# Conv pre-activation kernel (Hartley modes, then Sobel): edge sums one operation per chunk, half the pad cleared in pieces, one first-axis product moved

## The reference, cut to what matters

```python
# layer 0
x_ht = dht_2d(gn(x))                          # 128 x 128 Hartley transform, normalised per plane
out_modes = compl_mul2d(x_ht[:, :, :20, :20], weights1)   # sum over the input channels
x = x + idht_2d(zero_padded(out_modes))
# layer 1
g = gn(x)
gx, gy = depthwise_sobel(g)                   # 3 x 3, zero padding
x = x + sqrt(gx * gx + gy * gy + 1e-8)
```

## Time and profile before

| what | us |
|---|---|
| median of 3 executions | 2263.78 (2262.36 to 2263.88) |
| the profiled execution, its own time | 2263.11 |
| its span, first to last instruction | 2261.3 |
| PE busy | 2147.4 (95%) |
| ACT busy | 1960.1 (87%) |
| DVE busy | 1799.2 (80%) |
| POOL busy | 1631.3 (72%) |
| mean granted TensorE clock | 0.977 of full speed |

### The profile page before, as it was taken

How to read it: one execution, slowest core, us unless ns; L and a number is a source line. 1 busy time by engine, 2 the same in 40 slices (tenths; PEclk the granted TensorE clock), 3 DMA queues, 4 the chain that set the end, 5 groups by cost and what they waited for, 6 DMA issues and landing times.

```text
span 2261.3 us, 54772 instructions
## 1 busy us (share of the span) xinstructions
PE 2147.4 (95%) x20404; PEld 1564.9 (69%) x20404; DVE 1799.2 (80%) x2702; ACT 1960.1 (87%) x3688; POOL 1631.3 (72%) x931
## 2 busy tenths in 40 slices
PE   5999999999992789999999999999999999999998
PEld 4888888888882656666666666666666666666665
DVE  4888888888887558877877877877887887887777
ACT  5988889888884369899899899899899989989998
POOL 4777777677667257777777777777777777777776
PEclk9999999999996779999999999999999999999999
DMA  7777777777774216666566666666666666656664
GB/s 214 216 204 211 205 207 207 206 207 208 201 188 84 75 57 189 176 196 193 176 195 188 181 192 187 186 182 192 186 186 187 191 182 193 193 176 190 199 190 137
DMA packets 808226, 414.62 MB, mean 183 GB/s; under 512 B 20784, under 2 KB 807216, under 8 KB 807344
## 3 DMA queue, kind: packets, MB, share of 16 engines
q1 hardware_dynamic: 807984, 411.30, 63.5%
HBM read 277.00 MB, written 134.22 MB: 182 GB/s over the span
## 4 chain that ended last, share of the span: by engine, by line
PE 64%; DVE 0%; issue 0%; ACT 0%; POOLq 0%; POOL 0%; DVEq 0%; ACTq 0%
PE g_ps L1107 45%; PE y_ps L1099 10%; PE v_ps L1087 7%; PE v_ps L1075 1%; PE g_ps L1127 0%; DVE xbuf L1259 0%; DVE coef L1275 0%; POOLq L930 0%; POOL p_lo L1048 0%; ACT coef_t L1215 0%; PE y_ps L1127 0%; DVE g_ps L1265 0%; ACT g_ps L1180 0%; ACT p_hi L1161 0%; ACT g_ps L1186 0%
## 5 line engine op out<-in xcount | busy, mean ns | idle before, releaser
L1107 PE MATMUL g_ps<-p_hi,stencil 128*128 128x512 f32 x2048 | 851.2, 416 | 2.5 <-POOL p_lo L1048 2.5
L1048 POOL TENSOR_TENSOR p_lo<-pairs,p_hi 128x1032 fp32r<-128x1032 f32 x256 | 617.0, 2410 | 313.8 <-ACT p_hi L1161 313.8
L1107 PE MATMUL g_ps<-p_lo,stencil 128*128 128x512 f32 x2048 | 818.0, 399 | 0.0
L1107 PEld LDWEIGHTS g_ps<-p_hi,stencil 128*128 128x128 f32 x2048 | 386.9, 189 | 278.1 <-POOL p_lo L1048 143.4
L1265 DVE TENSOR_TENSOR g_ps<-gx,g_ps 128x512 f32<-128x512 f32 x512 | 350.5, 696 | 255.9 <-ACT g_ps L1180 255.2
L1043 POOL TENSOR_TENSOR pairs<-xbuf 128x1032 f32<-128x1032 f32 x256 | 488.1, 1907 | 33.5 <-DVE xbuf L1259 13.7
L1287 DVE SCALAR_TENSOR_TENSOR xbuf<-xbuf,rows,g_ps 128x256 f32<-128x256 f32 x1024 | 439.6, 478 | 38.2 <-ACT g_ps L1186 29.5
L1107 PEld LDWEIGHTS g_ps<-p_lo,stencil 128*128 128x128 f32 x2048 | 387.4, 189 | 81.9
L330 POOL TENSOR_TENSOR m_lo<-xbuf,m_hi 128x512 fp32r<-128x512 f32 x256 | 305.2, 1195 | 178.9 <-ACT m_hi L444 178.9
L1186 ACT ACTIVATE g_ps<-g_ps,rows 128x256 f32<-128x256 f32 x1024 | 408.1, 448 | 24.6 <-DVE g_ps L1265 6.0
L527 DVE TENSOR_REDUCE rows<-square 128x1024 f32 (+1 forms) x256 | 310.8, 1214 | 90.7 <-ACT square L476 88.6
(11 more groups left out here) (124 smaller groups left out, 2316.4 us busy)
## 6 DMA issues: line engine op xcount, KB each, us to landing
xbuf<-x SPq DMA_DIRECT2D x256, 512.0 KB, 5.2
xbuf<-x SPq DMA_DIRECT2D x512, 256.0 KB, 3.2
out<-xbuf SPq DMA_DIRECT2D x512, 256.0 KB, 2.9
wmix<-weights SPq DMA_DIRECT2D x8, 800.0 KB, 11.9
second_sb<-second SPq DMA_DIRECT2D x1, 1230.0 KB, 8.3
mats_sb<-mats SPq DMA_DIRECT2D x1, 704.0 KB, 6.5
first_sb<-first SPq DMA_DIRECT2D x1, 32.0 KB, 5.6
```

Source lines behind the costliest of these rows:

```text
L1048: nc.gpsimd.tensor_tensor(p_lo[:, r % 2, :, 0:W + 1], pairs[:, r % 2, :, 0:W + 1], p_hi[:, r % 2, :, 0:W + 1].bitcast(FP32), ALU.subtract) ...
L1107: mm = nc.tensor.matmul(g_ps[h][:, axis], stencil[:, m, :], p[:, r % 2, 4 * h:4 * h + 4, o:o + W], start=n == 0, stop=n == len(todo) - 1)
```

## The change: what it does

In pass 1 DVE's `edges` is cut into its four operations, and each is issued at a chunk of its own: the first product at k = 2, the second at k = 3, the sum at k = 4, the add at k = 5, always behind the sums of the chunk before. Each product now raises `edge_muled`, so the counts that PE, ACT and DVE wait for are doubled. For the last tile the four still run one behind the other.

In pass 2 POOL clears only half 0 of `coef_t` before its work and half 1 in four pieces of 128 x 736, each ahead of `low` in steps 1 to 4; DVE's wait at the start is for one clear, and PE waits for all five before the first `second_axis` that reads half 1. And in step 0 alone, PE's `first_axis` of step 3 is issued behind the stencil instead of ahead of it.

```diff
--- before.py
+++ after.py
@@ -377,7 +377,7 @@
             def edges(i, par):
 
                 pe.wait_ge(edge_in, (i + 1) * CHUNKS)
-                pe.wait_ge(edge_muled, i + 2)
+                pe.wait_ge(edge_muled, 2 * i + 4)
                 for a, flip in enumerate(("flip_half", "flip2_neghalf")):
                     mm = nc.tensor.matmul(edge_ps[:, a], mat(flip), edge[:, par, :, :, a],
                                           start=a == 0, stop=True, skip_group_check=True)
@@ -457,7 +457,7 @@
 
             def tile(i, par):
                 act.wait_ge(pe_second, i + 1)
-                act.wait_ge(edge_muled, i + 1)
+                act.wait_ge(edge_muled, 2 * i + 2)
                 if is_first(i):
                     high(i, 0, 0)
                 for k in range(CHUNKS):
@@ -490,26 +490,29 @@
         @block.vector
         def _(dve):
             dve.sem_inc(mirrored, 2)
-            dve.sem_inc(edge_muled, 2)
+            dve.sem_inc(edge_muled, 4)
             dve.sem_inc(summed, 2)
             dve.wait_ge(consts_in, 32)
             nc.vector.tensor_copy(flips[:, 0, :], mat("flip")).then_inc(flips_ready, 1)
             nc.vector.tensor_copy(flips[:, 1, :], mat("flip2_neg")).then_inc(flips_ready, 1)
 
-            def edges(i, par):
-
-                dve.wait_ge(pe_edge, i + 1)
-                for a in range(2):
-                    mul = nc.vector.tensor_tensor(edge_prod[:, :, :, a], edge[:, par, :, :, a],
-                                                  edge_ps[:, a], ALU.mult)
-                mul.then_inc(edge_muled, 1)
-                dve.wait_ge(edge_muled, i + 3)
-                nc.vector.tensor_reduce(edge_sum[:], edge_prod[:].rearrange("p n b a -> p n (b a)"),
-                                        axis=AX.X, op=ALU.add).then_inc(edge_summed, 1)
-                dve.wait_ge(edge_summed, i + 1)
-                dve.wait_ge(chunk_done, (i + 1) * CHUNKS)
-                row = rows[:, 0, bass.ds(i, 1), :]
-                nc.vector.tensor_tensor(row, row, edge_sum[:].unsqueeze(1), ALU.add).then_inc(tile_done, 1)
+            def edges(i, par, part):
+
+
+                if part < 2:
+                    if part == 0:
+                        dve.wait_ge(pe_edge, i + 1)
+                    nc.vector.tensor_tensor(edge_prod[:, :, :, part], edge[:, par, :, :, part],
+                                            edge_ps[:, part], ALU.mult).then_inc(edge_muled, 1)
+                elif part == 2:
+                    dve.wait_ge(edge_muled, 2 * i + 6)
+                    nc.vector.tensor_reduce(edge_sum[:], edge_prod[:].rearrange("p n b a -> p n (b a)"),
+                                            axis=AX.X, op=ALU.add).then_inc(edge_summed, 1)
+                else:
+                    dve.wait_ge(edge_summed, i + 1)
+                    dve.wait_ge(chunk_done, (i + 1) * CHUNKS)
+                    row = rows[:, 0, bass.ds(i, 1), :]
+                    nc.vector.tensor_tensor(row, row, edge_sum[:].unsqueeze(1), ALU.add).then_inc(tile_done, 1)
 
             def sums(i, k):
 
@@ -536,12 +539,13 @@
                         sums(i, k - 1)
                     elif not is_first(i):
                         sums(i - 1, CHUNKS - 1)
-                    if k == 2 and not is_first(i):
-                        edges(i - 1, 1 - par)
+                    if 2 <= k < 6 and not is_first(i):
+                        edges(i - 1, 1 - par, k - 2)
 
             over_tiles(dve, tile)
             sums(TILES - 1, CHUNKS - 1)
-            edges(TILES - 1, 1)
+            for part in range(4):
+                edges(TILES - 1, 1, part)
             dve.wait_ge(stats_pe, TILES)
             for a, name in enumerate(("diffs", "s2")):
                 nc.vector.tensor_copy(small[:, SMALL.index(name), :], stat_ps[:, a])
@@ -1033,8 +1037,7 @@
 
         @block.gpsimd
         def _(pool):
-            for par in range(2):
-                nc.gpsimd.memset(coef_t[:, par, :, NB:PITCH], 0.0).then_inc(cleared, 1)
+            nc.gpsimd.memset(coef_t[:, 0, :, NB:PITCH], 0.0).then_inc(cleared, 1)
             nc.gpsimd.memset(xpad[:, :, :, 0:W + 2:W + 1], 0.0).then_inc(padded, 1)
 
             def neighbours(i, r):
@@ -1048,7 +1051,12 @@
                 nc.gpsimd.tensor_tensor(p_lo[:, r % 2, :, 0:W + 1], pairs[:, r % 2, :, 0:W + 1],
                                         p_hi[:, r % 2, :, 0:W + 1].bitcast(FP32), ALU.subtract).then_inc(lo_ready, 1)
 
+            def clear(n):
+                nc.gpsimd.memset(coef_t[:, 1, 32 * n:32 * (n + 1), NB:PITCH], 0.0).then_inc(cleared, 1)
+
             def step(i, r):
+                if 1 <= at(i, r) <= 4:
+                    clear(at(i, r) - 1)
                 if not beyond(i, r + 1):
                     low(i, r + 1)
                 if not beyond(i, r + 3):
@@ -1080,6 +1088,8 @@
                     pe.wait_ge(coef_out, (pair_of(i, r) + 1) * TGRP + after_group + 1)
                 if not before(i, r, 1):
                     pe.wait_ge(v_out, at(i, r))
+                if at(i, r) == PSTEPS:
+                    pe.wait_ge(cleared, 5)
                 for m in range(2):
                     p0 = r % PSTEPS * 4 + 2 * m
                     for q in range(2):
@@ -1140,7 +1150,7 @@
             def step(i, r):
                 if not beyond(i, r + 4):
                     second_axis(i, r + 4, group(i, r - 1) if r else None)
-                if not beyond(i, r + 3):
+                if not beyond(i, r + 3) and not before(i, r, 1):
                     first_axis(i, r + 3)
                 pe.wait_ge(lo_ready, at(i, r) + 1)
                 across(i, r, 0)
@@ -1149,6 +1159,8 @@
                     transposes(i, r, group(i, r))
                 down(i, r, 0)
                 down(i, r, 1)
+                if before(i, r, 1):
+                    first_axis(i, r + 3)
 
             over_steps(step)
 
@@ -1302,7 +1314,7 @@
                 n = min(4, NB - 4 * g)
                 V.tensor_copy(coef_t[:, 0, :, 4 * g:4 * g + n].rearrange("k p j -> k j p"),
                               tile0_ps[g % len(tile0_ps)][:, 0:n, :]).then_inc(tile0_out, 1)
-            dve.wait_ge(cleared, 2)
+            dve.wait_ge(cleared, 1)
             dve.wait_ge(tile0_act, TGRP // 2)
             dve.wait_ge(tile0_out, TGRP - TGRP // 2)
             dve.sem_inc(coef_out, TGRP)
```

## The result

The changed kernel takes 2242.12 us (median of 4 executions, 2241.47 to 2242.79) against 2263.31 for the kernel before in the same comparison: ratio 0.9907, 95% interval 0.989 to 0.9924. The profiled execution has a span of 2240.9 us against 2261.3, 20.4 us less. The forecast was 2247.6 with a range from 2243.3 to 2253.5: right in sign, but 5.5 us too high and 1.2 us outside the range.

What follows compares the result with a forecast made beforehand. PE was taken to bound both passes, stalled in pass 1 by DVE's late mirror products and at pass 2's start by DVE's coefficients. 13.7 + 2.1 + 0.4 = 16.2 us off gave 2247.6 us, range 2243.3 to 2253.5.

Steps and rivals of the forecast that it cites:

- (a): Rival, pass 1: the add still stalls PE from its new place, 8.7 us comes back, 2256.3 us; chance 0.09.
- (c): Rival, pass 1: DVE has no room, all 2.8 us per tile fall on PE, slower at 2290 us; chance 0.02.
- (d): Rival, pass 1: the edges' stall has another cause and stays; only pass 2's start gains, 2261.3 us; chance 0.03.
- (b): Rival, early pass 2: PE's low-clock stretch moves or changes length, 2243 or 2250 us; chance 0.12 beyond 1.5 us either side.
- Part one: Pass 1: spreading DVE's edge operations removes PE's stall in 13 tiles, 13.7 us gained, ends 13.0 and 14.5.
- costs nothing: Pass 1, tile 2: its short add leaves a lump of some 1.8 us, claimed to cause PE no stall.
- I take 1.05: Pass 1: gain per tile in us, between 1.04 against tile 2 and a little more; times 13 tiles.
- Part two: Start of pass 2: clearing only half first lets DVE's coefficients finish sooner, 2.1 us gained, ends 1.8 and 2.3.
- 0.49 alone: Start of pass 2: L1275 would take 0.49 us undisturbed instead of 2.78, taken from L1277's row.
- everything behind moves by it: Start of pass 2: transposes, evictions and prologue come earlier by the 2.1 us taken for the clear.
- Part three: Pass 2, step 0: first_axis behind the stencil, 0.4 us gained, between 0.2 lost and 1.4 gained.
- nothing in these rows ties the rise to one pause: Pass 2, step 0: reason for taking 0.4 us, nearer the lower end, for the move's clock effect.

Runs made afterwards that it cites:

- e5: Kernel before, its edge lump kept at k = 2, but the edge sum written to PSUM so the add has one SBUF input: 2250.49 us, ratio 0.9949.
- e11: Changed kernel with DVE's edge sum done twice more per tile, at k = 6 and 7, into an unread buffer: 2242.45 us, ratio 0.9911.
- e1: Kernel before with only the edge operations of pass 1 spread, pass 2 as before: 2246.23 us, ratio 0.9931.
- e4: Changed kernel, but POOL clears both halves whole behind DVE's coefficients and stencil copies, none in steps 1 to 4: 2239.22 us, ratio 0.9903.
- e3: Kernel before with only first_axis of step 3 moved behind the stencil of step 0: 2260.48 us, ratio 0.9997.
- e9: Kernel before, unchanged, run once more for a second profile: span 2259.9 us.
- e12: The late-clear kernel e4 with first_axis of step 3 back ahead of the stencil of step 0: 2239.57 us, ratio 0.99.

## Why the prediction was wrong

**What held.** Pass 1's stall is two waits per tile in 13 tiles, caused by a lump on DVE that is too large because the add waits for POOL: without that wait (e5) 12.2 of the 15.1 us are gained with the lump left in place, and more work in pieces costs nothing (e11). The Trainium skill's rule on the shared port pair (SBUF — State Buffer, Who interferes with whom) agrees with e5: with one input in SBUF the add takes 0.29 us beside POOL's reading operation, with two 1.3. Rivals (a), (c) and (d) did not occur; (b) did in part, on the fast side. The clears hide in POOL's idle time, and the new wait for `centre` is 0.97 us where 0.93 was worked out.

**Part one, 13.7 us: mis-sized, it is 15.1** (573.8 to 558.7, and 558.6 in e1). The failing step is the lump of tile 2 that "costs nothing", and with it "I take 1.05". Tile 2's 4.88 us, taken as the interval without a stall, held a rest of one: the free interval is 4.81, and e5, where every tile is like tile 2, shows 4.89 to 5.00. So the stall was 1.11 us in each tile that has it and 0.07 in tile 2, 14.5 in all up to tile 15. Another 0.9 us is in the interval behind chunk 6, which the prediction did not price: in the kernel before it is 4.67 us in most tiles but 4.76, 4.88, 4.89 and 5.03 in four. The two intervals around the start of a tile give 0.3 us back in sum. Each profile of a kernel with the 2.8 us lump or that of e5 has some such intervals behind chunk 6 (sums 0.4 to 1.2 us), those without it at most 0.03 us. PE waits for no engine there: in the longest one, of tile 12, the time is lost within the chunk's own 64 first-axis products, with PEld idle for 0.24 us and no releaser shown. Why the lump brings them is open.

**Part two, 2.1 us: 2.36 in its own stage.** L1287 starts 780.24, while the small clear is shown from 780.04 for 0.49 us, and takes 0.50. That is 0.09 us more than the same operation in e4 with no clear beside it (0.41), so it was hardly held. The price of "0.49 alone" was itself not free of POOL: L1277 lay beside the small clear, and its successor now takes 0.41. 2.28 and 0.08 make the 2.36, just above my upper end of 2.3. The step that failed is "everything behind moves by it": the transposes behind also became 0.8 us shorter, at a higher granted clock behind PE's shorter pause. The price of the clock in rival (b) was worked out for step 0 and the products before it alone, and the transposes, the first thing behind the pause, were left out.

**Part three, 0.4 us: it is 1.1** (means of the table). Both ends of the working, 0.2 lost and 1.4 gained, stood there, and I chose by "nothing in these rows ties the rise to one pause". That choice is the failing step. In all profiles the rise comes 4.7 to 6.7 us after the end of the last pause that PE's timeline shows ahead of it (0.55 us long, 0.96 in e3), with the move or without it. The move takes that pause away, and the rise comes 13.0 to 13.7 us after the first second_axis in the seven profiles with it, against 16.3 to 17.7 in the seven without. That the move brings the rise forward is shown; that it does so through the pause, and not through the order of the products, is argued from these distances. The Trainium skill (TensorE: Matmul & The Clock Gate, What's actually happening) has it that the place of the rise varies from run to run. It does: the kernel before has it 17.7 and 16.9 us behind the first second_axis in its two profiles. But the move shifts it by 3.7 us on average, so the conclusion that this part's sign is chance was wrong.

**The rest, 0.9 us,** the wide products, is the clock of that one execution, as e9 shows: luck, and no part of the change. Over all profiles they take 6.6 to 7.7 us in kernels with the edges in one lump and 6.5 to 7.4 in those with the edges spread. Such differences also lie in the anchor. The kernel before took between 2260.26 and 2264.22 us in 19 executions, median 2262.0, where the forecast started from a median of three, 2263.78. It put the median 0.67 us above the profiled execution, and for the changed kernel it lies 0.59 below (2242.12 against 2242.71).

The sum by stages is 15.1 + 2.4 + 0.8 + 1.1 = 19.4 us, of which 16.2 were forecast. Of the miss of 5.5 us, 3.2 are these terms, 1.0 the wide products and rounding, and 1.3 the place of the medians. The terms alone would have left the time at 2244.4, inside the range; that it fell outside took the scatter of single executions as well. The prediction's "about 4 us to each side" does not follow from its bounds either: 14.5, 2.3 and 1.4 add up to 18.2, only 2.0 beyond the forecast, and the 19.4 lies outside them.

**What stays open:** the intervals behind chunk 6, what in the move brings the clock's rise forward, and whether the move is still worth its 0.9 us in time once the clears are late (e4 against e12).

## What to carry to other kernels

Look for the longest piece of work that an engine puts between two products its neighbour waits for, rather than for its total: here 2.8 us in one lump cost 1.1 us per tile, the same in two or four pieces nothing, and 1.3 us more per tile spread out also nothing. An operation that is several times longer than its shape warrants should be laid beside the other engines' rows; moving POOL's clears behind DVE's copies (e4) beat splitting them, by 2.9 us (e12 against e11, side by side). When a stall is priced against an undisturbed case, check that the case is free of the stall itself, and when a pause of PE becomes shorter, price what runs behind it at both clocks.

## What the runs showed of the hardware that was not expected

A DVE add with both inputs in SBUF took 1.00 to 1.41 us when it began behind the start of a POOL operation that reads SBUF, and 0.29 us at the same place with one input in PSUM (e5). DVE's scaling of `modes` into `coef` took 2.44 and 2.78 us beside POOL's large memsets, 0.50 beside the small one, and 0.38 and 0.41 without them (e4). The granted clock in the transposes was 0.66 to 0.73 of full after PE's pause of 7.25 us, 0.73 to 0.79 after 4.89 and 1.00 after 3.15.
